# A mixture-of-experts stage on one NeuronCore: each expert's weighted tile projected down by itself, instead of sums of two made on GpSimd

## The reference, cut to what matters

```python
def _L2_ffn_ref(tokens, gate_w, expert_w, expert_b, combine_w):
    logits = jnp.einsum('bsh,eh->bse', tokens, gate_w)
    probs = jax.nn.softmax(logits, axis=-1)
    top2_w, top2_idx = jax.lax.top_k(probs, 2)
    ...
    expert_out = jax.nn.silu(jnp.einsum('nh,edh->ned', flat, expert_w) + expert_b[None, :, :])
    gathered = jnp.take_along_axis(expert_out, flat_idx[:, :, None], axis=1)
    mixed = jnp.sum(gathered * flat_w[:, :, None], axis=1)
    out = jnp.einsum('bsh,dh->bsd', mixed.reshape(B, S, H), combine_w)
...
x = x + jnp.tanh(g_ffn[2]) * _L2_ffn_ref(_layernorm(x, axis=-1), ...)
```

## Time and profile before

| | |
|---|---|
| median of 3 runs | 1268.76 us (1267.93 to 1269.71) |
| the profiled execution | 1269.89 us |
| its span on the engines | 1268.1 us |
| TensorE, VectorE, ScalarE, GpSimd busy in it | 1142.7, 741.2, 702.3, 415.7 us |

### The profile page before, as it was taken

The page is one execution under the profiler, slowest core; times in us unless marked ns, Lnnn a source line. Parts: engine busy times, 40 slices in busy tenths (PEclk is TensorE's granted clock), DMA queues, the critical chain, the costliest instruction groups (busy, mean ns, idle before and its releaser), DMA issues. The chain is left out here.

```text
span 1268.1 us, 24927 instructions
## 1 busy us (share of the span) xinstructions
PE 1142.7 (90%) x9793; PEld 844.3 (67%) x9793; DVE 741.2 (58%) x1589; ACT 702.3 (55%) x1284; POOL 415.7 (33%) x601
## 2 busy tenths in 40 slices
PE   1879799699999999999998789979869997999998
PEld 0668357578888888888885556654536664466667
DVE  5858646455556556566561479974638994622224
ACT  2578541265666656666665256766346775644440
POOL 3200001133332323444444334421543532644441
PEclk9889799899999999999999899999979998999999
DMA  4500000100000000000000000000000000000000
GB/s 171 196 1 1 1 1 1 67 1 1 2 1 2 1 2 1 2 1 2 1 2 1 1 2 2 2 2 1 1 1 2 2 2 1 1 1 9 10 1 17
DMA packets 6529, 16.31 MB, mean 13 GB/s; under 512 B 1312, under 2 KB 3568, under 8 KB 5520
## 3 DMA queue, kind: packets, MB, share of 16 engines
q1 hardware_dynamic: 6416, 14.74, 3.2%
HBM read 13.69 MB, written 1.05 MB: 12 GB/s over the span
## 5 line engine op out<-in xcount | busy, mean ns | idle before, releaser
L1188 POOL TENSOR_TENSOR work<-work 128x1024 f32<-128x1024 f32 x64 | 121.3, 1896 | 275.8 <-DVE work L1281 275.8
L1268 DVE TENSOR_REDUCE work<-psum 128x8 f32<-128x1024 f32 x64 | 78.0, 1219 | 95.5 <-PE psum L1077 95.5
L1211 ACT ACTIVATE work<-work 128x1024 f32<-128x1024 f32 x64 | 67.4, 1053 | 98.3 <-DVE work L1272 98.3
L1279 DVE TENSOR_REDUCE work<-work 128x8 f32<-128x1024 f32 x64 | 77.4, 1209 | 70.3 <-ACT work L1211 70.3
L1615 PEld LDWEIGHTS psum<-w_down,work 128*128 128x128 f32 x768 | 99.5, 191 | 24.5 <-issue 22.0
L957 ACT ACTIVATE work<-psum 128x512 f32<-128x512 f32 x128 | 72.8, 596 | 62.5 <-PE psum L836 61.6
L1615 PE MATMUL psum<-w_down,work 128*128 128x128 f32 x768 | 100.6, 275 | 0.7 <-DVE x L1716 0.7
L995 DVE TENSOR_REDUCE work<-psum 128x8 f32<-128x1024 f32 x64 | 75.4, 1219 | 33.2 <-PE psum L822 33.2
L1708 DVE TENSOR_TENSOR work<-psum,big 128x512 f32<-128x512 f32 x69 | 47.3, 690 | 81.0 <-PE psum L1590 79.2
L836 PEld LDWEIGHTS psum<-ident,work 128*128 128x128 f32 x512 | 56.5, 141 | 43.1 <-issue 27.9
L1272 DVE TENSOR_TENSOR work<-psum,work 128x1024 f32<-128x1024 f32 x64 | 78.4, 1225 | 6.4
(11 more groups left out here) (336 smaller groups left out, 2646.0 us busy)
## 6 DMA issues: line engine op xcount, KB each, us to landing
x<-in_x SPq DMA_DIRECT2D x1, 1024.0 KB, 4.9
ctx_tok<-in_ctx SPq DMA_DIRECT2D x1, 1024.0 KB, 6.9
ctxt<-in_ctxt SPq DMA_DIRECT2D x1, 1024.0 KB, 10.5
mask<-in_mask SPq DMA_DIRECT2D x1, 1024.0 KB, 7.4
w_down<-in_down SPq DMA_DIRECT2D x1, 1024.0 KB, 6.6
ctx_tok<-in_g SPq DMA_DIRECT2D x1, 1024.0 KB, 5.5
big<-in_u SPq DMA_DIRECT2D x1, 1024.0 KB, 7.5
out<-x SPq DMA_DIRECT2D x4, 256.0 KB, 2.2
```

Of the source, the lines that this page charges most:

```text
L1188: pool.tensor_tensor(prob[:, u % 2, h, :], prob[:, u % 2, h, :], rinv[:, u % 2, h].unsqueeze(2).broadcast_to([P, 8, P]), ALU.mult)\
L1211: act.activation(p, p, ACT.Exp).then_inc(S["exp"], 1)
L1268: dve.tensor_reduce(nmax[:, u % 2, h], s, AX.X, ALU.max, negate=True).then_inc(S["max"], 1)
L1279: dve.tensor_reduce(rsum[:, u % 2, h], prob[:, u % 2, h, :], AX.X, ALU.add).then_inc(S["sum"], 1)
```

## The change

The switch `one_down` is gone from `feed_forward`, and with it `sum_pair` and its semaphore. `f2` now takes the path of the other stages: `down(n)` waits for `made` of its own tile and projects that tile, so 32 downs stand where 16 stood, and GpSimd keeps only the reciprocal roots. LAG goes from 4 to 2, the lags (ROOT, NORM, TURN) from (4, 7, 8) to (1, 4, 5), and `h3` has 4 slots in place of 8. A new switch `three` keeps for `f2` what `one_down` also set: three PSUM banks for `up`, the place of the routing's turn and that of its exponential. The other stages are written as before.

```diff
--- before.py
+++ after.py
@@ -1497,22 +1497,22 @@
         dve.tensor_tensor(parts[:, :, 2, :], low, parts[:, :, 1, :], ALU.subtract).then_inc(S["parts"], 1)
 
 
-def feed_forward(k, tag, sub, tiles, function, ahead, lags, one_down=False, routing=None, spare=(), bias=None,
-                 requantise=None, joint=False, on_act=False):
+def feed_forward(k, tag, sub, tiles, function, ahead, lags, routing=None, spare=(), bias=None,
+                 requantise=None, joint=False, on_act=False, three=False):
 
 
 
     nc, bank = k.nc, k.bank
     J = len(tiles)
     N = NG * J
-    LAG = 4 if one_down else 2
+    LAG = 2
     ROOT, NORM, TURN = lags
     routed = routing is not None
     second = tiles[0][2] is not None
     last_sub = sub == 7
     a = Arena(k)
     r = Route(k, a, tag + "r", **routing) if routed else None
-    H = J if one_down else 3
+    H = 4 if three else 3
     h3 = a.take(H * GT, "p (n c) -> p n c", n=H) if routed else None
     u = a.take(2 * GT, "p (n c) -> p n c", n=2) if second else None
     if not last_sub:
@@ -1524,7 +1524,7 @@
     ring = [one[:, n * GT:(n + 1) * GT] for one in spare for n in range(NG)][:R]
     ring += [a.take(GT) for _ in range(R - len(ring))]
     S = {n: k.sem(f"{tag}_" + n) for n in
-         ("up", "up2", "act", "second", "prod", "sel", "made", "summed", "down", "comb", "biased", "added",
+         ("up", "up2", "act", "second", "prod", "sel", "made", "down", "comb", "biased", "added",
           "stated", "aggr", "chain", "rstd", "normed", "turned", "kept", "stored")}
     weighted = [t[3] is not None for t in tiles]
     W = sum(weighted)
@@ -1534,7 +1534,7 @@
         return n // J * W + sum(weighted[:n % J + 1])
 
     weighted_tiles = [n for n in range(N) if weighted[n % J]]
-    up_banks = (bank[0], bank[1], bank[3]) if one_down else (bank[0], bank[1])
+    up_banks = (bank[0], bank[1], bank[3]) if three else (bank[0], bank[1])
     B = len(up_banks)
     y = (bank[6], bank[6] if second else bank[2])
     turned = bank[7] if second or routed else bank[3]
@@ -1592,17 +1592,6 @@
 
             def down(n):
                 g, j = divmod(n, J)
-                if one_down:
-                    if n % 2 == 0:
-                        return
-                    pe.wait_ge(S["summed"], n // 2 + 1)
-                    if j == 1 and g >= 2:
-                        pe.wait_ge(S["added"], g - 1)
-                    for b in range(GB):
-                        mm = pe.matmul(y[g % 2][:, b * P:(b + 1) * P], h3[:, (n - 1) % H, b * P:(b + 1) * P], tiles[j][4],
-                                       start=j == 1 and b == 0, stop=j == J - 1, skip_group_check=True)
-                    mm.then_inc(S["down"], 1)
-                    return
                 if weighted[j]:
                     pe.wait_ge(S["made"], made(n))
                     h = h3[:, (made(n) - 1) % H, :]
@@ -1631,7 +1620,7 @@
                 r.logits(pe)
             for n in range(ahead):
                 up(n)
-                if routed and n == (0 if one_down else 1):
+                if routed and n == (0 if three else 1):
                     r.turn(pe)
             if routed:
                 r.turn_back(pe, 0)
@@ -1676,7 +1665,7 @@
             if routed:
                 r.scores(act)
             for n in range(ahead):
-                if n == 4 and one_down:
+                if n == 4 and three:
                     r.exponential(act)
                 activate(n)
             if routed:
@@ -1701,16 +1690,13 @@
                 dve.wait_ge(S["sel"], c + 1)
                 wait_ready(dve, n)
                 if c >= H:
-                    if one_down:
-                        dve.wait_ge(S["down"], (n - H) // 2 + 1)
-                    else:
-                        dve.wait_ge(S["down"], weighted_tiles[c - H] + 1)
+                    dve.wait_ge(S["down"], weighted_tiles[c - H] + 1)
                 dve.tensor_tensor(h3[:, c % H, :], bank[4 + c % 2][:, :], ring[n % R], ALU.mult)\
                    .then_inc(S["made"], 1)
 
             def add(g):
                 xg = k.x[:, g * GT:(g + 1) * GT]
-                dve.wait_ge(S["down"], (g + 1) * (J // 2 if one_down else J))
+                dve.wait_ge(S["down"], (g + 1) * J)
                 if bias is not None:
                     dve.wait_ge(S["biased"], 1)
                 dve.scalar_tensor_tensor(out=xg, in0=y[g % 2][:, :], scalar=gate, in1=xg, op0=ALU.mult,
@@ -1756,12 +1742,6 @@
             def multiply(n):
                 pool.wait_ge(S["second"], n + 1)
                 pool.tensor_tensor(ring[n % R], ring[n % R], u[:, n % 2, :], ALU.mult).then_inc(S["prod"], 1)
-
-            def sum_pair(n):
-
-                one, other = h3[:, (n - 1) % H, :], h3[:, n % H, :]
-                pool.wait_ge(S["made"], n + 1)
-                pool.tensor_tensor(one, one, other, ALU.add).then_inc(S["summed"], 1)
 
             def reciprocal_root(n):
                 g0, g1 = roots[n]
@@ -1796,8 +1776,6 @@
                 for n in range(N):
                     multiply(n)
             for m in range(N + LAG + TURN + 1):
-                if one_down and m < N and m % 2:
-                    sum_pair(m)
                 for n, (_, g1) in enumerate(roots):
                     if not last_sub and m == last(g1 - 1) + ROOT:
                         reciprocal_root(n)
@@ -1932,7 +1910,7 @@
         if stages > 5:
             tiles = [(cut("ew2", j), k.cols[:, C_EB + j:C_EB + j + 1], None,
                       k.sels[:, j * P:(j + 1) * P], w["comb2"][:, :]) for j in range(8)]
-            k.stage(feed_forward, "f2", 5, tiles, ACT.Silu, ahead=12, lags=(4, 7, 8), on_act=True, one_down=True,
+            k.stage(feed_forward, "f2", 5, tiles, ACT.Silu, ahead=12, lags=(1, 4, 5), on_act=True, three=True,
                     spare=(k.big[0], k.big[2], k.negb),
                     routing=dict(E=8, groups=None, top_groups=None, top=2, kind="softmax", gate_w=w["gate2"]))
 
```

## The result

The changed kernel takes 1278.36 us (median of 4 runs, 1277.34 to 1279.35) against 1269.24 us (4 runs) on the same chip: a ratio of 1.0073, 95% interval 1.0056 to 1.0091. The forecast was 1278.2.

What follows compares the result with a forecast made beforehand. TensorE was taken to set f2's pace while there are ups, with waits and a lower clock behind them; laying f0's durations along f2 gave +9.36, taken as 9.4, so 1268.76 + 9.4 = 1278.2 us, range 1275.5 to 1281.

Steps and rivals of the forecast that it cites:

- A step with an up costs 1.97 us, and ten more downs stand there.: f2's steps with ups: 18 downs where 8 stood, so step 20, the first without an up, begins 8.6 us later.
- The waits that come with LAG = 2.: f2 behind the ups: select(28) 0.85 us late through VectorE, and TensorE waiting 0.74 us at group 2's turn.
- The waits and the slow clock that go.: f2's stretch 905.17 to 922.18: 6.5 us of waits and slow clock before, of which the changed kernel keeps 1.6.
- The tail costs nothing.: f2 from the last add on: statistics, root, normalising and turn as before, costed at nothing.
- The head of `a3` may give something back.: Rival, start of a3: if the clock rises as early as in a2, 1.1 us come back, +8.3, 1277.0; chance 0.2.
- What a down costs.: f2's downs: 0.89 us each, 111 ns a pair; the skill's 81 ns would make the change cost 5.6 us.
- The sum for the stage: f2's timeline laid out with f0's durations: last add at 931.54 in place of 922.18, +9.36 us.
- a balance of single durations: Check by work in f2: 14.6 us of added downs and turn less 4.9 of waits and slow clock, +9.7.

Runs made afterwards that it cites:

- e3: Changed kernel with the down of six tiles beside ups projecting one block of 128 tokens out of four: 1275.51 us, ratio 1.0046, stage 76.86 us.
- e5: Changed kernel with the down of six tiles beside ups done twice: 1286.37 us, ratio 1.0126, stage 86.12 us.
- e2: Changed kernel with a down per tile, but LAG = 4, eight h3 slots and lags (4, 7, 8) as before: 1277.84 us, ratio 1.0059, stage 79.46 us.
- e6: Changed kernel with TURN = 8 in place of 5 in f2: 1277.93 us, ratio 1.0058, stage 79.23 us.
- e7: Kernel before, sums on GpSimd kept, with TURN = 12 in place of 8 in f2: 1269.88 us, ratio 0.9999, stage 69.35 us.
- e8: Changed kernel run once more, unaltered: 1278.63 us, ratio 1.0074, stage 80.76 us.
- e4: Changed kernel with 16 unused sums of zeros put on GpSimd, at each odd tile: 1279.84 us, ratio 1.0070, stage 80.87 us.
- e1: Kernel before, with sums on GpSimd and LAG = 4, but lags (1, 4, 5) in f2: 1276.94 us, ratio 1.0055, stage 76.99 us.

## Why the prediction was right

- *A step with an up costs 1.97 us, and ten more downs stand there.* Right: step 20 came 8.6 us late as worked out. e3 and e5 show that the step follows the down's work linearly.
- *The waits that come with LAG = 2.* Right in this kernel: 0.78 us of idle (0.85 of delay) of the select and 0.77 of the turn, against 0.85 and 0.74. They could be read from `f0` since `f0` had the same order. Where the order differs by one turn (e2, e6) the same stall is half as long; that it depends on the turn I had not seen.
- *The waits and the slow clock that go.* Right: the stretch of downs runs at 1.00.
- *The tail costs nothing.* Right: from the last `add` to `a3` 940.30 - 931.43 = 8.87 us, before 8.86. The chain of a group took as long as forecast too: from the `add` of group 2 to its turn 927.84 - 921.00 = 6.84 us, against 6.83.
- *The head of `a3` may give something back.* It did: 945.67 - 940.30 = 5.37 us in place of 6.62, 1.25 where the rival had 1.1. But the time did not keep it. The first loads of `a3` lie 940.30 - 931.04 = 9.26 us apart in the two traces, the first of `f3` 9.04 and the ends 9.47. So the size of the rival was right, and its effect on the end was not. The rows show where it was lost. Behind its head, TensorE of `a3` stands idle for 3.7 us, and then does the same 107 matmuls up to the third pair of VectorE's reductions (954.39 before, 963.40 after). The idle stretch and the busy one, before and then after:

```profile
938.80:942.53 3.73, 0.00 (x1) 0.00 (x0) 3.63 (x4) 0.02 (x1) 2.78 (x4) 0.73 0.00 0
942.53:954.39 11.86, 11.37 (x107) 5.58 (x108) 6.94 (x7) 6.84 (x9) 2.72 (x3) 0.80 0.01 1
```

```profile
946.81:950.55 3.74, 0.01 (x2) 0.01 (x1) 3.64 (x4) 0.03 (x2) 3.74 (x5) 1.00 0.00 0
950.55:963.40 12.85, 12.38 (x107) 5.97 (x108) 6.94 (x7) 6.83 (x9) 2.93 (x4) 0.73 0.01 1
```

Before, a part of the low clock fell into the idle time (0.73 there), where it costs nothing; after, all of it fell on matmuls, and the same work took 12.85 - 11.86 = 0.99 us more. `f3` then took another 0.4 us (last section). That the forecast of the whole time came within 0.2 us is thus in part luck: the 1.25 us that the sum left out were lost again by a clock that it left out too. The sum for the stage, 9.36 against 9.40, did not need this luck.

- *What a down costs.* 0.89 us, 111 ns for a float32 pair, and not the 81 ns of the Trainium skill ("TensorE: Matmul & The Clock Gate", section "Back-to-back issue gap"); e3 and e5 confirm the trace's number.

## What to carry to other kernels

A sum of two operands on an idle engine ahead of a linear map halves the matmuls behind it, and is worth most of what these matmuls cost where TensorE sets the pace. Here 16 sums of 1.27 us on GpSimd, hidden while there were ups, stood against 16 x 0.89 = 14.2 us on TensorE; the stage without sums was 9.4 us longer and not 14.2, since behind the ups the kernel with sums had more waits and a low clock. An engine that is busier after a change, at a better clock, is no gain by itself. Where the program holds a stage of the same form as the changed one, its rows give step lengths and stalls together: they gave 9.36 us here, a balance of single durations 9.7, and 9.40 were measured. Work that waits for a long chain belongs behind the matmuls that don't need it (e6, e7; both for the stage, while e7's whole time did not show it), and short work that is ready, such as a turn, right where another engine is busy with a block of its own.

## What the runs showed of the hardware

**The moment at which the clock rises at the head of `f3` moves the time by up to 1.8 us.** The same `f3`, from its first gate load to the end, took 1268.1 - 1065.38 = 202.7 us in the kernel before, 1278.0 - 1076.20 = 201.8 in e6 and 1267.7 - 1064.23 = 203.5 in e7. The stretches hold its first 35 us, in the order before, e6, e7:

```profile
1065.50:1100.50 35.00, 35.00 (x89) 15.11 (x90) 23.24 (x122) 24.33 (x39) 21.86 (x17) 0.93 0.00 1
```

```profile
1076.00:1111.00 35.00, 34.77 (x93) 15.24 (x94) 23.29 (x122) 24.69 (x40) 22.20 (x17) 0.95 0.00 0
```

```profile
1064.00:1099.00 35.00, 34.74 (x87) 15.01 (x88) 22.86 (x122) 23.83 (x38) 20.93 (x16) 0.91 0.00 0
```

All ten traces have this order to within 0.05 us. The table gives `f3` and the mean clock in its first 10 us, in which TensorE is busy for at least 9.96 us in each of them:

| run | e2 | e5 | e6 | before | after | e8 | e4 | e3 | e1 | e7 |
|---|---|---|---|---|---|---|---|---|---|---|
| `f3`, us | 201.7 | 201.7 | 201.8 | 202.7 | 203.2 | 203.2 | 203.2 | 203.3 | 203.3 | 203.5 |
| clock | 0.85 | 0.85 | 0.84 | 0.76 | 0.71 | 0.71 | 0.70 | 0.69 | 0.70 | 0.68 |

Between the ends of the table the clock costs (0.85 - 0.68) x 10 = 1.7 us, and the times differ by 1.8. The later the clock rises behind the idle time between the two stages, the later the end. What sets the moment was not tried. A change worth 2 us in one stage can be hidden or doubled by this, and only the stage's own rows tell.

**A wait of TensorE is paid again by the clock.** In the kernel before, 3.0 us of waiting brought the following stretch to 0.75; in e1 two waits of 2.2 us brought it to 0.66 and 0.63. Waits of 0.8 us in the changed kernel and one of 1.68 in e7 left the clock at 1.00. Whether the length of the wait alone decides was not tried.
